# A graph network kernel: edge tables copied out of PSUM with group and side innermost, in place of the column

## The chip, the cores and the metric

The kernel runs on one core of one Trainium2 chip. The metric is the device time of one execution in microseconds (us). Three timed runs of the kernel before gave 2148.09, 2145.54 and 2143.85 us; the median is 2145.54 us.

The engines are called by the names that the profile uses: PE (matrix products), PEld (PE's weight loads), DVE (vector), ACT (scalar), POOL (GpSimd) and SP (which issues most DMAs).

## The reference, cut to what matters

Four graph layers run one after the other over 6250 nodes of 128 features, with a layer norm and a ReLU ahead of each. All of them sum over the same 206250 edges, sorted by destination:

```python
edge_index = jnp.stack([src, dst])
h = relu(layernorm(x)); x = x + L0(h, W1, b1, W2, b2, edge_weight, src, dst)   # weighted segment sum
h = relu(layernorm(x)); x = x + L1(h, edge_index, batch0, ...)                 # mean over incoming edges
h = relu(layernorm(x)); x = x + L2(h, x_clique, edge_index, W, b)              # mean of clique rows
h = relu(layernorm(x)); x = x + L3(h, edge_index, W_in, ..., W_out, b_out)     # gated update
# the sum over edges in each of them:
neighbor = jax.ops.segment_sum(edge_val[:, None] * x[edge_src], edge_dst, num_segments=N_NODES)
```

## The kernel before

The kernel does not gather a row for every edge. It builds the matrix of edge counts (and, for layer 0, of edge weights) between blocks of 128 nodes out of one-hot products on PE, writes the counts to DRAM, and multiplies the node rows by them. This has four parts in time: a setup, until about 146 us; the counting loop over 49 halves, until about 1174 us, which also finishes layer 0; the products of layers 1 and 2; and layer 3.

The change lies in the setup. Nodes are cut into groups of four (G). For every group there is a table entry for each edge, 128 edges from each of two sides (s = 0 counts from the group's first edge, s = 1 from its end). There are four tables, LO (low bits of the source), KEY (destination and high bits), WHI and WLO (the edge's weight in two f16 parts). They are made with the node group on the partitions and the edge along the row, and the counting loop wants the edge on the partitions. So `flip_groups` on PE multiplies every 128x128 square by the identity into PSUM, and `from_tab` copies it from PSUM (f32) to the table (f16). In PSUM, `p_tab[side]` lies as 7 groups x 2 sides x 128 columns, so one group and side is a run of 128 f32 (512 bytes). In the table the order is column n, then group g (13 of them, NGT), then side s: entries of one group and side that follow each other in n lie 13 x 2 f16, that is 52 bytes, apart.

The 13 groups go in two parts (TILES): part 0 has groups 0 to 6, part 1 has groups 7 to 12. `p_tab[0]` serves LO and WHI, which ACT copies (L1324, from the call ahead of `order_known` in the scalar block); `p_tab[1]` serves KEY and WLO, which DVE copies (L1722, `tables`). Each call of `from_tab` makes two copies: a small one of column 120 (14 elements a partition in part 0, 2 in part 1), and the main one of columns 0 to 119, with 120 x 7 x 2 = 1680 elements a partition in part 0 and 120 x 6 x 2 = 1440 in part 1. The small one is written with group and side as its only dimensions: it reads one f32 every 512 bytes and writes f16 in a row.

What sets the order around the change is code written by hand with semaphores. PE flips in the order LO, KEY, WHI, WLO of part 0, then the same of part 1 (L828). WHI may be flipped only when LO has been taken from `p_tab[0]` (`tab_taken0`), WLO only when KEY has been taken from `p_tab[1]` (`tab_taken1`), and so on in turns. ACT makes LO and WHI in f16 ahead (L1300, L1301), and has the layer norm of 24 blocks (L1317) between its two parts. DVE's list is: keys of part 0 (L1696 to L1702), KEY 0, WLO 0, keys of part 1, a check of the keys (L1708 to L1733), KEY 1, WLO 1, then `any_order` (L1736), and the semaphore `order_known`, which every engine waits for before it branches into the counting loop. POOL normalises the other 25 blocks (L731, L733); when it is done, SP stores the rows to DRAM (`node_rows`, L434).

Of the kernel before, what the change touches and what calls it, by code (L numbers as in the profile page):

```python
# [51 lines left out]
NGT = -(-NB * P // (G * P))  # L52
# [33 lines left out]
def build_gnn(nc, A, out):  # L86
    with ExitStack() as ctx:
# [209 lines left out]
        p_tab = [ps[:, n * 4 * TILE:n * 4 * TILE + 14 * P].rearrange("p (g s n) -> p g s n", g=7, s=2) for n in range(2)]  # L297
# [969 lines left out]
        def _(act):  # L1267
# [7 lines left out]
            def from_tab(write, tab, first, last, side):  # L1275

                full = NQUAD // NGT
                over = min(last, NQUAD - full * NGT) - first
                if over > 0:
                    write(tab[:, full * NGT * 2:].rearrange("p (g s) -> p g s", s=2)[:, first:first + over, :],  # L1280
                          p_tab[side][:, 0:over, :, full])
                t = tab[:, 0:full * NGT * 2].rearrange("p (n g s) -> p g s n", g=NGT, s=2)[:, first:last]
                return write(t, p_tab[side][:, 0:last - first, :, 0:full])

            act.wait_ge(sem("scan_ready"), 1)
            for g in SIGNED:
# [29 lines left out]
            for b in range(ACT_ROWS):  # L1316
                last = nc.scalar.activation(h0[:, b, :], h0[:, b, :], ACT.Relu, bias=shift0[:, b:b + 1],  # L1317
                                            scale=rstd0[:, b:b + 1])
            last.then_inc(sem("h0_ready"), 1)
            high_parts(1, *TILES[1])  # L1320
            for n, (first, last) in enumerate(TILES):
                for step, tab in ((0, LO), (2, WHI)):
                    act.wait_ge(sem("flipped"), n * 4 + step + 1)
                    from_tab(lambda t, v: nc.scalar.copy(t, v), tabs[tab], first, last, 0).then_inc(sem("tab_taken0"), 1)  # L1324
# [218 lines left out]
        def _(dve):  # L1543
# [139 lines left out]
            def from_tab(write, tab, first, last, side):  # L1683

                full = NQUAD // NGT
                over = min(last, NQUAD - full * NGT) - first
                if over > 0:
                    write(tab[:, full * NGT * 2:].rearrange("p (g s) -> p g s", s=2)[:, first:first + over, :],
                          p_tab[side][:, 0:over, :, full])
                t = tab[:, 0:full * NGT * 2].rearrange("p (n g s) -> p g s n", g=NGT, s=2)[:, first:last]  # L1690
                return write(t, p_tab[side][:, 0:last - first, :, 0:full])

            def keys(n, first, last):
                dve.wait_ge(sem(f"rec_in{n}"), 32 * (last - first))
# [24 lines left out]
            def tables(n, first, last):  # L1719
                for step, tab in ((1, KEY), (3, WLO)):  # L1720
                    dve.wait_ge(sem("flipped"), n * 4 + step + 1)
                    from_tab(lambda t, v: V.tensor_copy(t, v), tabs[tab], first, last, 1).then_inc(sem("tab_taken1"), 1)  # L1722
# [612 lines left out]
```

## Time and profile before

| what | value |
|---|---|
| timed runs, median | 2145.54 us |
| the profiled execution, its own time | 2161.86 us |
| its span on the core | 2159.9 us |
| granted PE clock, mean over the span | 0.96 |
| busy: PE, DVE, ACT, POOL | 1954.4, 1513.4, 1233.0, 140.3 us |
| share of the chain that ended last: PE, DVE, ACT | 81%, 6%, 5% |

The profiled execution took 16.3 us more than the median of the timed ones; its durations are read against its own span. Busy time is the time in which an engine has an instruction running; a busy PE is one whose queue of matmuls is not empty, and need not be at its peak. In the timeline, a row gives the start, the time, the engine, the line and the operation; rows of one line that follow each other are merged under the shape of the first (x2 means two instructions), and the bracket gives the idle time ahead and what ended it.

### The profile page before, as it was taken

How to read it: one execution, taken by the hardware profiler on the slowest of the kernel's cores; microseconds unless marked ns; L12 is line 12 of the kernel's file. 1: busy time of each engine (PE TensorE's matmuls, PEld its weight loads, DVE VectorE, ACT ScalarE, POOL GpSimd, SP SyncE). 2: the span in 40 equal slices, each digit the busy share in tenths (PEclk: the TensorE clock that was granted, in tenths of full speed). 3: DMA queues.
4: the chain of work that ended last, by engine and by line, in shares of the span. 5: the costliest groups of instructions: out<-in, count | busy, mean ns of one | idle time of the engine just before them, and what ended most of it. 6: DMA issues, size and time to landing. Idle time of an engine off the chain costs nothing.

```text
span 2159.9 us, 62665 instructions
## 1 busy us (share of the span) xinstructions
PE 1954.4 (90%) x22348; PEld 1769.7 (82%) x22393; DVE 1513.4 (70%) x3127; ACT 1233.0 (57%) x3189; POOL 140.3 (6%) x120
## 2 busy tenths in 40 slices
PE   1039999999999999999999899999999778999997
PEld 1039999999999999999999677777788766888854
DVE  8378888888888888888886666666887367100066
ACT  5456666666666666666665588888888543000043
POOL 4700000000000000000000000000000144000011
PEclk7559999999999999999999999999999989999999
DMA  8322222221222222121222433333487259998722
GB/s 229 91 61 96 74 101 91 83 100 73 100 73 101 84 91 100 73 100 73 100 77 103 164 140 132 134 130 136 159 316 257 69 163 348 369 315 300 267 83 77
DMA packets 184486, 304.21 MB, mean 141 GB/s; under 512 B 12642, under 2 KB 135959, under 8 KB 184175
## 3 DMA queue, kind: packets, MB, share of 16 engines
q1 hardware_dynamic: 180506, 290.74, 38.5%
q0 software_dynamic: 3904, 12.50, 1.9%
q8 instruction: 44, 0.72, 0.1%
q14 instruction: 32, 0.25, 0.0%
HBM read 202.70 MB, written 100.48 MB: 140 GB/s over the span
## 4 chain that ended last, share of the span: by engine, by line
PE 81%; DVE 6%; ACT 5%; issue 4%; DMA 2%; DVEq 1%; ACTq 0%; SPq 0%; POOLq 0%
PE ps L902 25%; PE ps L994 21%; PE ps L891 11%; PE ps L885 7%; PE ps L986 6%; PE ps L972 3%; PE ps L1183 2%; PE ps L1061 1%; ACT edge_area L1335 1%; PE ps L1158 1%; DMA hs<-node_rows 1%; PE ps L1069 1%; ACT edge_area L1288 1%; DMA edge_area<-x_stream 1%; DVE carry L1722 1%
## 5 line engine op out<-in xcount | busy, mean ns | idle before, releaser
L1335 ACT CAST edge_area<-ps 128x392 f16<-128x392 f32 x784 | 407.2, 519 | 393.1 <-PE ps L885 393.1
L902 PE MATMUL ps<-big,rows_area 128*128 128x128 f32 x4802 | 576.9, 277 | 0.0
L902 PEld LDWEIGHTS ps<-big,rows_area 128*128 128x128 f32 x4802 | 551.9, 192 | 0.0
L1341 ACT COPY big<-ps 128x392 f32<-128x392 f32 x784 | 416.9, 532 | 0.8 <-PE ps L891 0.5
L891 PE MATMUL ps<-edge_area 128*128 128x98 f16 x6272 | 416.7, 208 | 0.0
L1818 DVE TENSOR_TENSOR edge_area<-lo_pair,carry 128x1024 f16<-128x1024 f16 x392 | 269.2, 687 | 129.0 <-PE ps L891 125.4
L891 PEld LDWEIGHTS ps<-edge_area 128*128 128x128 f16 x6272 | 331.7, 97 | 0.0
L885 PE MATMUL ps<-edge_area 128*128 128x98 f16 x3136 | 276.3, 209 | 17.7 <-DVE edge_area L1824 11.0
L994 PE MATMUL ps<-big,agg 128*128 128x256 f16 (+1 forms) x2450 | 278.6, 271 | 0.0
L994 PEld LDWEIGHTS ps<-big,agg 128*128 128x128 f16 x2450 | 232.7, 98 | 25.3
L1819 DVE TENSOR_TENSOR edge_area<-cell_pair,carry 128x784 f16<-128x784 f16 x392 | 219.2, 559 | 0.0
L1824 DVE TENSOR_TENSOR edge_area<-edge_area,carry 128x784 f16<-128x784 f16 x392 | 219.0, 559 | 0.0
L1823 DVE TENSOR_TENSOR edge_area<-edge_area,carry 128x784 f16<-128x784 f16 x392 | 217.5, 555 | 0.1
L885 PEld LDWEIGHTS ps<-edge_area 128*128 128x128 f16 x3136 | 190.0, 98 | 33.6 <-ACT edge_area L1335 12.8
L1410 ACT ACTIVATE edge_area<-ps,edge_area 128x896 bf16<-128x896 f32 x175 | 167.0, 1003 | 75.4 <-PE ps L972 61.6
L1429 ACT ACTIVATE edge_area<-big 128x256 f16<-128x256 f16 (+1 forms) x504 | 201.0, 404 | 12.4 <-issue 2.6
L994 PE MATMUL ps<-big,rows_area 128*128 128x256 f16 (+1 forms) x1862 | 198.4, 270 | 0.0
L994 PEld LDWEIGHTS ps<-big,rows_area 128*128 128x128 f16 x1862 | 178.1, 98 | 20.1
L2070 DVE TENSOR_REDUCE out_part<-big 128x4 f32<-128x1024 f16 (+1 forms) x168 | 193.7, 1189 | 0.0
L2062 DVE TENSOR_TENSOR carry<-carry,ps 128x896 f32<-128x896 f32 x85 | 92.3, 1086 | 89.7 <-PE ps L986 89.7
L986 PE MATMUL ps<-edge_area 128*128 128x384 bf16 (+1 forms) x655 | 137.6, 351 | 3.6 <-DVE carry L2062 1.2
L2099 DVE TENSOR_SCALAR agg<-ps 128x256 f32 (+2 forms) x19 | 7.9, 418 | 180.2 <-PE ps L994 180.2
(253 smaller groups left out, 1793.1 us busy)
## 6 DMA issues: line engine op xcount, KB each, us to landing
big<-edge_counts SPq DMA_DIRECT2D x315, 448.0 KB, 5.2
edge_counts<-edge_area SPq DMA_DIRECT2D x49, 1568.0 KB, 5.6
agg<-edge_counts SPq DMA_DIRECT2D x21, 448.0 KB, 7.2
hs<-node_rows POOLq DMA_DIRECT2D x14, 448.0 KB, 4.3
edge_area<-x_stream SPq DMA_DIRECT2D x14, 448.0 KB, 4.3
node_rows<-rows_area SPq DMA_DIRECT2D x1, 3136.0 KB, 12.9
agg_s<-node_rows SPq DMA_DIRECT2D x49, 64.0 KB, 4.9
agg_s<-in_x SPq DMA_DIRECT2D x49, 64.0 KB, 1.8
```

Source lines behind the costliest of these rows:

```text
L885: last = mm(pair_of(p_count[s % 2], c), sources_of(slot, r, c), cells_of(oh_cell, slot, r, c), start=(c == 0), stop=(c == 3), skip_group_c ...
L891: last = mm(pair_of(p_weight[s % 4], c), sources_of(slot, r, c), cells_of(oh, slot, r, c), start=(c == 0 and oh is oh_whi), stop=(c == 3 a ...
L902: last = mm(p_sum, h0[:, n, :], w32[:, par, n, :], start=(n == 0), stop=(n == NB - 1))
L986: last = mm(p_mix[:, lo:hi], xc_plane[:, par, c, l, :], flipped[:, odd, c, lo:hi], start=(c == 0 and l == 0), stop=(c == parts - 1 and l = ...
L994: last = mm((p_block if l == 1 else p_even_odd)[par][:, 0:width, :], planes1[:, sh, p, :] if l == 1 else planes[:, p, sh, :], piece[:, par ...
L1335: nc.scalar.copy(store_slot[:, par, :, cols], p_count[s % 2]).then_inc(sem("count_taken"), 1)
L1341: nc.scalar.copy(w32[:, par, :, cols], p_weight[s % 4]).then_inc(sem("weight_taken"), 1)
L1429: last = nc.scalar.activation(unused[:, j, 0:width, :], piece[:, par, k, 0:width, j, :], ACT.Copy, accum_out=out_part[:, par, sh:sh + 1])
L1818: V.tensor_tensor(oh_src[:, slot], paired(lo_pair, P), lo.to_broadcast([P, 4, P, 2]), ALU.is_equal)
L1819: V.tensor_tensor(oh_cell[:, slot], paired(cell_pair, CELLS), key.to_broadcast([P, 4, CELLS, 2]), ALU.is_equal)
L1823: V.tensor_tensor(oh_whi[:, slot], oh_cell[:, slot], whi.to_broadcast([P, 4, CELLS, 2]), ALU.mult)
L1824: V.tensor_tensor(oh_wlo[:, slot], oh_cell[:, slot], wlo.to_broadcast([P, 4, CELLS, 2]), ALU.mult).then_inc(sem("onehots"), 1)
```

## The change

The main copy of `from_tab` takes its three dimensions in another order, on both engines that have it. Before, the column n is innermost: 120 f32 that lie in a row in PSUM are read, and each f16 is written 52 bytes after the one before it. After, group and side are innermost: an f32 is read every 512 bytes in PSUM, 14 of them (12 in part 1), and they are written as a run of 28 bytes (24 in part 1); then comes the next column, with the run 52 bytes further on. The elements, the bytes and the number of instructions are the same.

```diff
-                t = tab[:, 0:full * NGT * 2].rearrange("p (n g s) -> p g s n", g=NGT, s=2)[:, first:last]
-                return write(t, p_tab[side][:, 0:last - first, :, 0:full])
+                t = tab[:, 0:full * NGT * 2].rearrange("p (n g s) -> p n g s", g=NGT, s=2)[:, :, first:last, :]
+                return write(t, p_tab[side][:, 0:last - first, :, 0:full].rearrange("p g s n -> p n g s"))
```

The same two lines change in the scalar block (L1282 and L1283) and in the vector block (L1690 and L1691). No instruction changes its place. On DVE, in the setup between the keys of part 0 and those of part 1, the list differs only in the shape of the main copies (`carry` holds the tables, `ps` is PSUM):

```order
 L1702 SCALAR_TENSOR_TENSOR big<-edge_area,w_scale,big 128x1792
 L1722 CAST carry<-ps 128x14
-L1722 CAST carry<-ps 128x14x120
+L1722 CAST carry<-ps 128x120x14
 L1722 CAST carry<-ps 128x14
-L1722 CAST carry<-ps 128x14x120
+L1722 CAST carry<-ps 128x120x14
 L1696 TENSOR_SCALAR agg<-edge_area,first_key 128x256 x6
```

Nothing moved; eight copies in all (four on DVE, four on ACT) have this other shape.

## Rows read from the trace of the kernel before

**Rows 1.** Stretches: length, busy us of PE, PEld, DVE, ACT, POOL, PEclk, DMA share, GB/s.
```profile
100.00:141.00 41.00, 9.18 (x78) 8.22 (x78) 26.88 (x26) 28.98 (x9) 8.06 (x1) 0.54 0.28 79
141.00:146.00 5.00, 0.78 (x2) 0.49 (x2) 0.30 (x2) 0.00 (x0) 0.00 (x0) 0.50 0.03 7
170.00:1080.00 910.00, 904.58 (x12755) 891.50 (x12754) 794.97 (x1880) 570.33 (x1468) 0.00 (x0) 1.00 0.24 88
```

**Rows 2.** The timeline of the setup's end and the loop's first store, 98 to 166 us.
```profile
98.15 2.32 ACT L1301 ACTIVATE big<-edge_area,w_scale 128x1536 f16<-128x1536 f32 x1
100.39 7.64 ACT L1324 CAST carry<-ps 128x14 f16<-128x14 f32 x2
108.09 0.40 SPq L434 DMA_DIRECT2D node_rows<-rows_area  x1
108.17 3.08 PE L828 MATMUL ps<-ident,big 128*128 128x128 f16 x28 [20.76 <-ACT carry L1324]
109.86 7.67 ACT L1324 CAST carry<-ps 128x14 f16<-128x14 f32 x2 [1.83 <-PE ps L828]
111.29 7.70 DVE L1722 CAST carry<-ps 128x14 f16<-128x14 f32 x2 [14.08 <-PE ps L828]
117.68 1.44 PE L828 MATMUL ps<-ident,big 128*128 128x128 f16 x12 [6.43 <-ACT carry L1324]
121.64 2.31 DVE L1702 SCALAR_TENSOR_TENSOR big<-edge_area,w_scale,big 128x1536 f16<-128x1536 f32 x1
125.48 6.57 DVE L1722 CAST carry<-ps 128x2 f16<-128x2 f32 x2
132.20 1.44 PE L828 MATMUL ps<-ident,big 128*128 128x128 f16 x12 [4.77 <-DVE carry L1722]
133.67 6.57 DVE L1722 CAST carry<-ps 128x2 f16<-128x2 f32 x2 [1.62 <-PE ps L828]
145.99 0.69 DVE L1818 TENSOR_TENSOR edge_area<-lo_pair,carry 128x1024 f16<-128x1024 f16 x1 [3.40 <-issue]
165.38 0.40 SPq L454 DMA_DIRECT2D edge_counts<-edge_area  x1
```

**Rows 3.** Groups by line and shape, 0 to 140 us: the copies of the tables.
```profile
L1722 DVE CAST carry<-ps 128x1680 f16<-128x1680 f32 x2 | 15.3, 7628 | 0.0
L1324 ACT CAST carry<-ps 128x1680 f16<-128x1680 f32 x2 | 15.2, 7600 | 0.0
L1722 DVE CAST carry<-ps 128x1440 f16<-128x1440 f32 x2 | 13.0, 6501 | 0.0
L1722 DVE CAST carry<-ps 128x14 f16<-128x14 f32 x2 | 0.3, 162 | 14.1 <-PE ps L828 14.1
L1324 ACT CAST carry<-ps 128x14 f16<-128x14 f32 x2 | 0.3, 156 | 1.8 <-PE ps L828 1.8
L1722 DVE CAST carry<-ps 128x2 f16<-128x2 f32 x2 | 0.3, 154 | 1.6 <-PE ps L828 1.6
L1324 ACT CAST carry<-ps 128x2 f16<-128x2 f32 x2 | 0.3, 160 | 3.2 <-PE ps L828 3.2
```

**Rows 4.** Groups by line and shape: the nearest other copies, and two groups of the page.
```profile
L1300 ACT CAST big<-edge_area 128x1792 f16<-128x1792 f32 x1 | 2.6, 2636 | 4.7 <-DVE w_scale L1647 4.7
L1702 DVE SCALAR_TENSOR_TENSOR big<-edge_area,w_scale,big 128x1792 f16<-128x1792 f32 x1 | 2.7, 2669 | 1.6 <-ACT big L1301 1.6
L1410 ACT ACTIVATE edge_area<-ps,edge_area 128x896 bf16<-128x896 f32 x175 | 167.0, 1003 | 75.4 <-PE ps L972 61.6
L2062 DVE TENSOR_TENSOR carry<-carry,ps 128x896 f32<-128x896 f32 x85 | 92.3, 1086 | 89.7 <-PE ps L986 89.7
```

**Rows 5.** The DMA queues, 116 to 121 us: packets, MB, share of 16 engines.
```profile
q1 hardware_dynamic: 2373, 1.21, 84.8%
q8 instruction: 1, 0.02, 1.1%
```

**Rows 6.** DVE's instruction with the longest idle time put down to issue, 0 to 140 us.
```profile
L1639 DVE TENSOR_SCALAR hs<-hs 128x49 f32<-128x49 f32 x1 | 0.2, 191 | 8.3 <-issue 8.3
```

More of the change, by code:

```diff
@@ L1689, in from_tab @@
                           p_tab[side][:, 0:over, :, full])
-                t = tab[:, 0:full * NGT * 2].rearrange("p (n g s) -> p g s n", g=NGT, s=2)[:, first:last]
-                return write(t, p_tab[side][:, 0:last - first, :, 0:full])
+                t = tab[:, 0:full * NGT * 2].rearrange("p (n g s) -> p n g s", g=NGT, s=2)[:, :, first:last, :]
+                return write(t, p_tab[side][:, 0:last - first, :, 0:full].rearrange("p g s n -> p n g s"))
             def keys(n, first, last):
```

## The prediction
> **What bounds the kernel now.** I read the page first, then the stretches, then the timeline of the stretch in which the changed lines run. From 170 to 1080 us PE is busy 904.58 of 910 us at a granted clock of 1.00 (the level of 2.4 GHz) [rows 1]: the counting loop is PE's, and the change has no instruction in it. From 100 to 141 us no engine is full: PE 9.18, DVE 26.88, ACT 28.98 us of 41 [rows 1]. A stretch like this is a chain of waits between engines, and a microsecond taken from a link of it is a microsecond of the end, as everything after it starts by one semaphore. So the question is which copies are links.
>
> The timeline gives them [rows 2]. ACT copies LO 0 at 100.39 for 7.64 us; PE, idle for 20.76 us and released by this copy, flips WHI 0 and WLO 0 (28 matmuls, 3.08 us, to 111.25); DVE, idle for 14.08 us, copies WLO 0 at 111.29 for 7.70 us, to 118.99; DVE makes and checks the keys of part 1 until 125.48 (6.49 us); it copies KEY 1 (6.57 us, to 132.05); PE flips WLO 1 (12 matmuls from 132.20, 1.44 us); DVE copies WLO 1 at 133.67 for 6.57 us, to 140.24. Then come `order_known`, the branch, and the first one-hot of the loop at 145.99, 5.75 us later. Four of the eight main copies are links, with 7.64 + 7.70 + 6.57 + 6.57 = 28.48 us. The other four (KEY 0, WHI 0, LO 1, WHI 1) lie beside them.
>
> **What the change costs and brings, per copy.** The copy of 1680 elements takes 7628 ns on DVE and 7600 on ACT, that of 1440 takes 6501 [rows 3]. The slope between the DVE sizes is (7628 - 6501) / 240 = 4.70 ns an element; over the whole copy it is (7628 - 154) / 1680 = 4.45, with 154 ns as the fixed part (the copy of 2 elements). Both engines have the same slope, so it is not the engine's arithmetic; ACT copies out of PSUM in a row at (1003 - 156) / 896 = 0.95 ns and DVE at (1086 - 154) / 896 = 1.04 ns [rows 3, 4]. The reading of the slow copies is in a row too. What is left as the cause is the write of a lone f16 every 52 bytes, and that is what the edit removes.
>
> What it adds is a read of PSUM at one f32 every 512 bytes. The trace does show this read, once: the small copy of column 120 has just this pattern, 14 elements read 512 bytes apart and 28 bytes written in a row. It takes 162 ns on DVE against 154 for 2 elements, and 156 against 160 on ACT [rows 3]. That is 8 ns for 12 elements more, 0.7 ns each, and nothing on ACT. A step that cost 4.45 ns would have shown 53 ns. It is a short sample, and a queue could hide a cost in it, so I bound the rate from both sides: 0.95 to 1.04 ns as the floor (copies in a row), and 4.45 ns as the upper end (the row of the slow pattern itself). Between them lie the copies that read SBUF one f32 every 12 bytes: (2636 - 156) / 1792 = 1.38 ns on ACT, (2669 - 154) / 1792 = 1.40 on DVE [rows 4]. I take the floor, since the small copy is the nearest row and stands there. Below the floor I expect nothing: no copy out of PSUM in these rows is quicker than 0.95 ns an element, and the 0.7 of the small one comes from a difference of 8 ns.
>
> The new pairs, each with the small copy and its handover (0.04 us on ACT, 7.64 - 7.60; 0.07 on DVE, 7.70 - 7.63): LO 0 on ACT 0.156 + 1680 x 0.95 ns + 0.04 = 1.79; WLO 0 on DVE 0.154 + 1680 x 1.04 ns + 0.07 = 1.97; KEY 1 and WLO 1 0.154 + 1440 x 1.04 ns + 0.07 = 1.72 each. Sum 7.20 us, against 28.48: **21.3 us less** on the chain. In general the four links hold 6240 elements, so each nanosecond an element is worth 6.24 us, and the gain is about 6.24 x (4.45 - r).
>
> The Trainium skill has a rule that speaks against this much: its page "Vector Engine (DVE) Microarchitecture Reference" (section 5.2, Measured stream behaviour on trn2) says that a source that hops every element streams at 1.73 ns, not 1.05, and a destination that hops at 1.71, or 2.5 at a small step. It speaks of 32-bit words in SBUF. By it the gain is 6.24 x (4.45 - 1.73) = 17.0 us. This case's trace disagrees with it on the old pattern (4.45 ns for a hopping f16 destination), and the small copy's 0.7 ns speaks against it on the new one, in a sample of 14.
>
> **Do other links take over?** With LO 0 done at 102.18, the flips end at 105.4, WLO 0 at 107.4; keys and check are relative to it and end at 113.9, KEY 1 at 115.6, WLO 1 runs from 117.2 to 119.0. What else must be there: the WHI parts that DVE's keys use are made by 100.5 (ACT L1301), ahead of LO 0 on ACT; WHI 0 is copied by about 105.8, LO 1 by 109.2; the keys are there for PE at about 110.1 (before, 121.64, where L1702 begins, 2.65 us after WLO 0), so KEY 1 and WHI 1 are flipped by 113.2, ahead of 113.9 when DVE wants KEY 1, and WHI 1 is copied by 114.8, ahead of 119.0. KEY 0 sits in DVE's wait for the flips of WLO 0 (14.08 us idle), so its gain is worth nothing. The slack of the nearest one (KEY 1 flipped at 111.7 against 113.9) is 2 us, and holds.
>
> POOL's share of the layer norm and SP's store of the rows don't move: the store is issued at 108.09 [rows 2] and its packets still fill the DMA queues in most of 116 to 121 us [rows 5]. Before, the end of the chain came 19 us after that; now it comes 2 us before it. Who waits for the store is SP, whose first work in the loop was at 165.38 us [rows 2] and will be near 144; PE wants the normalised rows in the second half of the loop, which begins about then. Neither waits. What remains is the branch: the loop's code has to be fetched, by DMA, about 2.5 us after `order_known`, near 121.5, just behind the store. The first one-hot had 3.40 us of issue ahead of it with empty queues [rows 2]; the store's last packets could add to that, and DVE once stood 8.3 us for issue earlier in the setup [rows 6]. That is the upper end of what may be given back here, nothing is the lower one; the store should be through, so I charge 0.3.
>
> The sum for the profiled execution: 2161.86 - 21.3 + 0.3 = 2140.9 us. It lies 16.3 us above the median of the timed runs; the setup's chain has nothing that depends on that difference, so the same 21.0 us come off the median: 2145.5 - 21.0 = 2124.5 us.
>
> **Rivals.**
> 1. The read hop costs something: 1.4 ns an element, like the reads of every 12 bytes [rows 4], up to 2.5. For it: the sample that speaks against it has 14 elements, and runs of 28 bytes start at odd multiples of 4 bytes. Gain 6.24 x (4.45 - 1.4) = 19.0 at one end and 12.2 at the other: 2126.5 to 2133.3 us. The skill's 1.73 falls in here, as said.
> 2. The two steps are alike: PSUM read at 512 bytes costs as much an element as the scattered write did, 4.45 ns. The two engines' equal slopes would fit a memory's limit of either kind. Against: 53 ns would have shown in the small copy. Gain 0: 2145.5 us.
> 3. Slower: the bank of PSUM changes with every fourth element now (512 bytes each, 2 KB a bank), and a read that hops costs more than the write did. It decides from 4.45 ns on; at 6 ns the chain grows by 6.24 x 1.55 = 9.7 us, to 2155.2. Against it, again the small copy, which crosses the banks in the same way.
> 4. The copies do fall to 2 us, but the start of the loop is held by something that doesn't move: the fetch of the loop's code stands behind the row store. Price: the loop starts not at 124.8 but by the stall of [rows 6] later, up to 8.3 us: 2127 to 2133 us.
>
> **How the numbers follow.** Forecast 0.72 (2121 to 2127); rival 1 0.13; rival 4 0.07; rival 2 0.05; rival 3 0.03. A difference of under 0.2% (4.3 us) can't be told from no change here; the forecast and rivals 1 and 4 all lie beyond it. So faster 0.92, within it 0.05, slower 0.03. The range: down to 2119 for a floor that is lower by the spread of timed runs (4 us between the three), up to 2132, which takes in most of rivals 1 and 4.
>
> **What would show it.** In the profile after, the main copies at L1324 and L1722 stand at 1.6 to 1.9 us; PE's idle time ahead of the flips of WHI 0 falls from 20.76 to about 15 us; the first one-hot stands near 124.8; the counting loop and all that follows keep their durations, 21 us earlier. Copies of 2.5 to 4.5 us say rival 1; 7 us, rival 2; short copies with a gap of over 4 us at issue ahead of the first one-hot, rival 4. The forecast is wrong if the small copy's read is no sample of the long one's, or if the loop does not keep its length.

## The result, and the profile after

The changed kernel took 2132.53 us (median of four runs, 2130.87 to 2134.58) against 2146.82 us for the kernel before (four runs, 2143.85 to 2149.35): a ratio of 0.9934, with a 95% interval of 0.9917 to 0.9952. It is faster, by 14.3 us. The forecast was 21.0 us less, 2124.5 us, with a range up to 2132.0. The sign was right, and so was what the copies would gain; a third of the gain is missing at the end. Three single executions in the runs further down took 4.1 to 6.8 ms and stand in no ratio.

The copies are not where it is missing. The groups by line and shape of the changed kernel, 60 to 118 us, as in [rows 3], with the two groups that the text comes to below:

```profile
L1696 DVE TENSOR_SCALAR agg<-edge_area,first_key 128x256 f32<-128x256 f32 x13 | 12.2, 1004 | 4.7 <-DMA edge_area<-edge_records,edge_idx 4.7
L733 POOL TENSOR_SCALAR rows_area<-rows_area 128x3200 f32<-128x3200 f32 x1 | 8.5, 8457 | 3.5 <-issue 3.5
L1722 DVE CAST carry<-ps 128x1680 f16<-128x1680 f32 x2 | 3.8, 1900 | 0.0
L1722 DVE CAST carry<-ps 128x1440 f16<-128x1440 f32 x2 | 3.3, 1648 | 0.0
L1324 ACT CAST carry<-ps 128x1680 f16<-128x1680 f32 x2 | 3.1, 1567 | 0.0
```

DVE's copy of 1680 elements went from 7628 to 1900 ns (forecast 1.90 us), that of 1440 from 6501 to 1648 (forecast 1.65), ACT's from 7600 to 1567 (forecast 1.75). A read of PSUM at 512 bytes costs nothing that these rows show: (1900 - 154) / 1680 = 1.04 ns an element on DVE, the rate of its copies in a row, and (1567 - 156) / 1680 = 0.84 ns on ACT, which is less than the 0.95 ns that the forecast took as the floor. The small copy of 14 elements was a good sample. Rivals 1 to 3 fall.

The first row is the surprise: L1696, the first step of DVE's keys, has a mean of 1004 ns. The timeline of the changed kernel, 84 to 118 us, answers to [rows 2]:

```profile
84.47 1.61 ACT L1324 CAST carry<-ps 128x14 f16<-128x14 f32 x2
86.23 3.03 PE L828 MATMUL ps<-ident,big 128*128 128x128 f16 x28 [17.43 <-ACT carry L1324]
89.30 1.99 DVE L1722 CAST carry<-ps 128x14 f16<-128x14 f32 x2 [16.49 <-PE ps L828]
91.20 9.90 DVE L1696 TENSOR_SCALAR agg<-edge_area,first_key 128x256 f32<-128x256 f32 x6
92.20 8.46 POOL L733 TENSOR_SCALAR rows_area<-rows_area 128x3200 f32<-128x3200 f32 x1 [3.46 <-issue]
105.92 1.72 DVE L1722 CAST carry<-ps 128x2 f16<-128x2 f32 x2
107.78 1.44 PE L828 MATMUL ps<-ident,big 128*128 128x128 f16 x12 [2.77 <-DVE carry L1722]
109.25 1.73 DVE L1722 CAST carry<-ps 128x2 f16<-128x2 f32 x2 [1.62 <-PE ps L828]
117.32 0.69 DVE L1818 TENSOR_TENSOR edge_area<-lo_pair,carry 128x1024 f16<-128x1024 f16 x1 [3.31 <-issue]
```

The six key instructions of part 1 took 9.90 us, and of the 13 in the kernel one took 8407 ns, where the median is 382:

```profile
L1696 DVE TENSOR_SCALAR agg<-edge_area,first_key x13: 371/382/8407, 63.0 to 100.7; 128x256 f32<-128x256 f32 x13
```

That one, the fifth of the six, begins at 92.40 and ends at 100.81 us. POOL's long ReLU (L733, 8.46 us) runs from 92.20 to 100.66. The trace also shows something else: everything here is earlier than in the profile of before by more than the copies explain. LO 0 starts at 84.47, not at 100.39, although nothing ahead of it was changed.

### The profile page after: what moved, and what is told of

The parts are those of the page before. It is cut to its first block, busy times and chain, and to the rows that moved or that the text cites. A ratio compares the mean times of both kernels' runs of the same rounds, so it can differ in the third digit from the quotient of the medians.

```text
span 2130.3 us, 62710 instructions
## 1 busy us (share of the span) xinstructions
PE 1955.3 (92%) x22393; PEld 1766.6 (83%) x22393; DVE 1498.5 (70%) x3127; ACT 1210.8 (57%) x3189; POOL 140.0 (7%) x120
## 4 chain that ended last, share of the span: by engine, by line
PE 81%; DVE 5%; ACT 4%; issue 3%; DMA 3%; POOL 1%; DVEq 1%; ACTq 0%; POOLq 0%; SPq 0%
PE ps L902 26%; PE ps L994 21%; PE ps L891 11%; PE ps L885 7%; PE ps L986 6%; PE ps L972 3%; PE ps L1183 2%; POOL edge_area L724 1%; PE ps L1061 1%; ACT edge_area L1335 1%; PE ps L1158 1%; DMA hs<-node_rows 1%; PE ps L1069 1%; ACT edge_area L1288 1%; DMA edge_area<-x_stream 1%
## 5 line engine op out<-in xcount | busy, mean ns | idle before, releaser
L986 PE MATMUL ps<-edge_area 128*128 128x512 bf16 (+1 forms) x700 | 148.0, 354 | 1.2 <-DVE carry L2062 1.2
```

The lines of the kernel that those rows point to most:

```text
L986: last = mm(p_mix[:, lo:hi], xc_plane[:, par, c, l, :], flipped[:, odd, c, lo:hi], start=(c == 0 and l == 0), stop=(c == parts - 1 and l = ...
```

## The experiments

**The kernel before, profiled again.** The same program was run and profiled four more times, to see what the setup of a 2146 us run looks like.

> The kernel before, unchanged, profiled a second time. Theory 1 (the keys of part 1 now meet POOL's long ReLU): the first profile of before had 23 us of DVE issue gaps at L1637 to L1645 that the timed runs do not have, so layer-norm scales come at about 58 us instead of 81; the chain is then set by the record gathers (landed about 80), LO 0 starts about 84.5, WLO 0 ends about 103, the keys of part 1 take about 6.5 us because POOL's L733 ended at about 100.7, and the first one-hot stands at about 130; L1696 of part 1 at 0.4 us each. Theory 2 (the time is given back at the branch or later, not at the keys): the keys of part 1 take as long as in the changed kernel, about 14 us, or the first one-hot stands at 138 or later. Time 2146 us in both.

> The kernel before, for its profile beside the kernels of this call. Theory 1: if its time is near 2146 us, layer-norm scales come at about 58 us without issue gaps, LO 0 starts near 84.5, WLO 0 ends near 103 when POOL's long ReLU is over (100.7), all L1696 are under 0.6 us, and the first one-hot stands near 130. Theory 2: an L1696 of several us is there too, so the ReLU is no new wait of the change. If its time is near 2162 us, the profile is as the first one.

> The kernel before, for its profile beside the kernels of this call; as for before_third: beside times near 2146 us the first one-hot near 130 with all L1696 under 0.6 us (theory 1), or with one of several us (theory 2).

> The kernel before, for its profile. Theory 1: beside times near 2146 us the first one-hot near 130, all L1696 under 0.6 us; theory 2: one L1696 of several us. Beside times near 2162 us as before_third.

Measured: 2162.22, 2161.41, 2162.41 and 2146.15 us. The setup is found in two conditions, whatever the kernel, and kernels that ran side by side were always in the same one (on one and the same chip both were met at different times). In the one, DVE waits for issue again and again from L1637 to L1645, as in [rows 6], and the layer-norm scales come at about 80 to 83 us: I call it *late scales*. It is that of the profile on which the prediction rests. In the other the scales come at 58 us: *early scales*. It is that of the timed runs. The timeline of before with early scales (before_fifth), 57 to 131 us:

```profile
57.75 0.21 DVE L1645 SCALAR_TENSOR_TENSOR hs<-hs 128x49 f32<-128x49 f32 x1
84.37 7.63 ACT L1324 CAST carry<-ps 128x14 f16<-128x14 f32 x2
92.18 8.31 POOL L733 TENSOR_SCALAR rows_area<-rows_area 128x3200 f32<-128x3200 f32 x1 [3.46 <-issue]
95.33 7.75 DVE L1722 CAST carry<-ps 128x14 f16<-128x14 f32 x2 [16.94 <-PE ps L828]
102.65 2.06 DVE L1696 TENSOR_SCALAR agg<-edge_area,first_key 128x256 f32<-128x256 f32 x6
109.58 6.56 DVE L1722 CAST carry<-ps 128x2 f16<-128x2 f32 x2
117.77 6.57 DVE L1722 CAST carry<-ps 128x2 f16<-128x2 f32 x2 [1.62 <-PE ps L828]
130.07 0.69 DVE L1818 TENSOR_TENSOR edge_area<-lo_pair,carry 128x1024 f16<-128x1024 f16 x1 [3.38 <-issue]
```

Here the keys of part 1 begin at 102.65, two microseconds after the ReLU's end (100.49), and take 2.06 us. So before, they never met it: with late scales neither, where the ReLU ended at 108.06 and the keys began at 118.59. The first one-hot stands at 130.07, as expected. DVE's waits for issue account for the late scales: 21.9 us of them from L1637 to L1645 in the first profile, none in before_fifth, and scales 23.5 us apart (81.28 and 57.75). What makes them come at some times and not at others was not found.

**The changed kernel in both conditions.**

> The changed kernel, unchanged, beside the others. The last four runs showed a kernel before at 2162 us with DVE waiting for issue at L1637 and L1639 (layer-norm scales at 82 us), where the result's runs had 2146 us and no such waits (scales at 58 us). Theory 1 (what the change gives depends on where POOL's long ReLU lies against the keys of part 1): beside a before of 2162 us the gain is the full sum of links less the last 1 us of the ReLU, 20 to 21 us (2141.5 us), with all L1696 under 0.6 us or one of about 1.2; beside a before of 2146 us it is 13 to 15 us (2132.5 us), with one L1696 of about 8 us. Theory 2 (about 7 us are given back wherever the copies are short): 14 us in both.

> The changed kernel once more. Theory 1: beside a before near 2162 us it gains 20 to 21 us (2141.5 us), the keys of part 1 meeting only the last microsecond of POOL's ReLU; beside one near 2146 us again 13.5 us (2132.5 us). Theory 2: 14 us in both.

Measured: with early scales 2132.89 us against 2146.55 (0.9936, interval 0.9922 to 0.9950), 13.7 us; with late scales 2142.06 against 2163.18 (0.9900, 0.9883 to 0.9916), 21.1 us. The second is the forecast's gain. That it agrees to a tenth is luck, as its interval is some 7 us wide, but the first one-hot moved by as much, 20.8 us (146.72 in before_fourth, 125.96 here). In the trace of after_third, 100 to 126 us, the keys begin in the ReLU's last microsecond (it ends at 108.65) and lose 0.6 us to it (2.62 us against 2.01 in before_fourth):

```profile
100.34 8.31 POOL L733 TENSOR_SCALAR rows_area<-rows_area 128x3200 f32<-128x3200 f32 x1 [3.46 <-issue]
107.68 2.62 DVE L1696 TENSOR_SCALAR agg<-edge_area,first_key 128x256 f32<-128x256 f32 x6
115.13 1.71 DVE L1722 CAST carry<-ps 128x2 f16<-128x2 f32 x2
125.96 0.69 DVE L1818 TENSOR_TENSOR edge_area<-lo_pair,carry 128x1024 f16<-128x1024 f16 x1 [3.38 <-issue]
```

**The ReLU twice.** The changed kernel, with (`...` marks what is cut from a line)

```diff
-            nc.gpsimd.tensor_scalar(h0[:, ACT_ROWS:NB, :], ..., 0.0, None, ALU.max).then_inc(sem("h0_ready"), 1)
+            nc.gpsimd.tensor_scalar(h0[:, ACT_ROWS:NB, :], ..., 0.0, None, ALU.max)
+            pool.drain()
+            nc.gpsimd.tensor_scalar(h0[:, ACT_ROWS:NB, :], ..., 0.0, None, ALU.max).then_inc(sem("h0_ready"), 1)
```

> The changed kernel with POOL's long ReLU (L733) done twice over; the second pass changes no value. Theory 1: DVE's L1696 of part 1 stands still until the second pass is over, so the whole kernel is 8 to 9 us slower than after_again beside it, and one L1696 of 8 us (before of 2162 us) or of 16 us (before of 2146 us) is seen. Theory 2 (the long L1696 was a wait for gathered records or for DVE's own pipe, not POOL): POOL is 20 us off the chain, so no change.

Measured: 2142.23 us, 9.3 us over after_again, which ran beside it (early scales); the first one-hot stands at 125.81 against 116.83. DVE's keys (here L1698) stand for both passes:

```profile
91.62 17.90 DVE L1698 TENSOR_SCALAR agg<-edge_area,first_key 128x256 f32<-128x256 f32 x6
92.47 8.31 POOL L733 TENSOR_SCALAR rows_area<-rows_area 128x3200 f32<-128x3200 f32 x1 [3.46 <-issue]
100.94 8.44 POOL L735 TENSOR_SCALAR rows_area<-rows_area 128x3200 f32<-128x3200 f32 x1 [0.15 <-issue]
```

DVE's keys wait for one semaphore that POOL has a part in, that of the gathers, and these were issued and landed earlier: the last was issued at 77.02 us in the changed kernel, and in keys_early, below, the same six instructions are done at 82.77. Nothing ties them to the ReLU. So it is the instructions themselves that exclude each other: two stood for 8.4 us each, one beside either pass, and one got through in the gap of 0.15 us between the passes. This settles the cause. It does not hold for every instruction of DVE. Its copies out of PSUM keep their length beside the same ReLU, 7.75 us at 95.33 in before_fifth above, and in keys_early:

```profile
94.75 8.31 POOL L733 TENSOR_SCALAR rows_area<-rows_area 128x3200 f32<-128x3200 f32 x1 [3.46 <-issue]
95.69 1.72 DVE L1722 CAST carry<-ps 128x2 f16<-128x2 f32 x2 [1.62 <-PE ps L828]
```

In the Trainium skill, "SBUF — State Buffer" (section SBUF: two separate sides) says that VectorE and GpSimd share a port pair, which a VectorE instruction takes only in a two-port mode or with two SBUF inputs, and that whichever starts first keeps it for the whole instruction while the other fully blocks. The trace agrees with the block: 8407 ns of DVE beside 8457 ns of POOL. In which mode L1696 ran, no run here shows.

**The layer norm's share off POOL.** The changed kernel, with POOL's L731 and L733 taken out and done by DVE behind KEY 0:

```diff
+                    if n == 0 and step == 1:
+                        for b in range(ACT_ROWS, NB):
+                            V.tensor_scalar(h0[:, b, :], h0[:, b, :], rstd0[:, b:b + 1], shift0[:, b:b + 1], ALU.mult, ALU.add)
+                        dve.drain()
+                        V.tensor_scalar(h0[:, ACT_ROWS:NB, :], ..., 0.0, None, ALU.max).then_inc(sem("h0_ready"), 1)
```

> The changed kernel with POOL's 25 blocks of layer norm and its long ReLU (L731, L733) moved to DVE, right behind KEY 0, where DVE is idle for 16 us; result the same. Theory 1: L1696 of part 1 back at 0.4 us each, keys of part 1 in about 6.5 us instead of 14.6, first one-hot near 109.5 instead of 117.3, time 2124.5 us, which is what was forecast for the change. Theory 2: the keys stay slow, or what they gain is lost at the branch; 2132.5 us.

> The changed kernel with POOL's share of the layer norm and its long ReLU moved to DVE behind KEY 0, a second time, since the first run stood beside a before of 2162 us, where the keys meet no ReLU. Theory 1: beside a before of 2146 us it is 7.5 to 8.5 us under the changed kernel, 2124.5 to 2125 us, which is the forecast for the change; no L1696 over 0.6 us, first one-hot near 109. Theory 2: 2132.5 us.

> The changed kernel with POOL's blocks and ReLU on DVE. Theory 1: beside a before near 2146 us 2124.5 to 2125 us, 8 us under the changed kernel; beside one near 2162 us within 1.5 us of the changed kernel, since there is next to nothing of the ReLU to meet there. Theory 2: it is 7 us or more under the changed kernel in both, or in neither.

> The changed kernel with POOL's blocks and ReLU on DVE. Theory 1: beside a before near 2146 us 2124.5 to 2125 us, 21.5 us under before and 8 us under the changed kernel; theory 2: 2132.5 us. Beside a before near 2162 us 2142 to 2143 us a fourth time.

> The kernel before with the same move of POOL's blocks and ReLU to DVE. Theory 1: before, the keys of part 1 come after the ReLU's end, so there is nothing to win: within 1 us of before (DVE's extra 8.5 us lie in its idle time ahead of WLO 0). Theory 2 (the move helps by itself, for instance by the earlier store of rows or by less sharing of a port elsewhere): several us under before.

Measured with late scales: 2143.86, 2142.25 and 2143.14 us, the last beside after_third's 2142.06: nothing to win there. With early scales (norm_on_dve_4): 2127.74 us against 2146.12 (0.9910, interval 0.9895 to 0.9924), 5.2 us under after_again (whose before had 2146.55), where 8 were expected. The same edit on the kernel before gave 2164.29 against 2162.66 (1.0013, 1.0004 to 1.0022), late scales: nothing won, and 1.6 us lost where at most 1 was expected. The trace of norm_on_dve_4 (DVE's keys at L1690, its copies at L1716):

```profile
79.40 1.83 DVE L1721 TENSOR_SCALAR rows_area<-rows_area 128x3200 f32<-128x3200 f32 x1
91.55 1.89 DVE L1690 TENSOR_SCALAR agg<-edge_area,first_key 128x256 f32<-128x256 f32 x6
98.26 1.72 DVE L1716 CAST carry<-ps 128x2 f16<-128x2 f32 x2
108.99 0.69 DVE L1818 TENSOR_TENSOR edge_area<-lo_pair,carry 128x1024 f16<-128x1024 f16 x1 [3.28 <-issue]
```

The whole gain is back at the start of the loop: 130.07 - 108.99 = 21.1 us before before_fifth, against the forecast's 21.3 for the links. What is left of the way is longer, though: from the first one-hot to the end of the span 2126.0 - 109.0 = 2017.0 us, against 2129.8 - 116.8 = 2013.0 in after_again. The counting loop is not where: from its first one-hot to its last it takes 1020.5 us in both. The difference opens in layer 3, at POOL's first additions there and at DVE's L2222, which waits for them. Here are these rows of after_again, then of norm_on_dve_4 (where POOL's lines lie 6 higher up):

```profile
1717.69 2.09 POOL L787 TENSOR_TENSOR big<-big,shift 128x896 f32<-128x896 f32 x1 [0.84 <-issue]
1722.12 1.09 DVE L2222 TENSOR_TENSOR big<-big 128x896 f32<-128x896 f32 x1 [0.36 <-POOL big L790]
```

```profile
1713.83 2.08 POOL L781 TENSOR_TENSOR big<-big,shift 128x896 f32<-128x896 f32 x1 [4.10 <-issue]
1718.25 1.09 DVE L2222 TENSOR_TENSOR big<-big 128x896 f32<-128x896 f32 x1 [3.62 <-POOL big L784]
```

POOL stands 4.10 us for issue ahead of that addition, not 0.84, and DVE 3.62 us for POOL, not 0.36: 3.3 of the 4.0 us. Every profile in which POOL's two lines are taken out has 4.10 there (seven, before_norm_on_dve and the two with keys early among them), and every other has 0.84. So the edit pays for its 7.8 us in the setup with some 3 us in layer 3; why POOL's issue takes longer there was not found.

**One engine at a time.**

> Only ACT's two lines changed (LO and WHI), DVE's copies as before. Theory 1: LO 0 is 6.0 us shorter, but then the keys of part 1 begin near 97 and stand still until POOL's long ReLU ends at 100.7; net gain 2 to 3 us, 2144 us. Theory 2 (no meeting of keys and ReLU): the gain is the whole 6.0 us of the link, 2140.5 us.

> Only DVE's two lines changed (KEY and WLO), ACT's copies as before. Theory 1: WLO 0, KEY 1 and WLO 1 give 5.7 + 4.8 + 4.8 = 15.3 us, of which 3 to 4 us are lost as the keys of part 1 begin near 97.4 and wait for POOL's long ReLU to end at 100.7; net 12 us, 2134.5 us, so that both halves together (12 + 2.5) are about what the whole change gave, 14.3 us, and not the 21.3 us of the sum of links. Theory 2: 15.3 us, 2131.5 us, no slower than the whole change.

Measured, both with late scales (before 2162.32 us): only ACT 2156.21 us (0.9973, 0.9963 to 0.9983), 6.1 us; only DVE 2154.15 us (0.9967, 0.9956 to 0.9978), 8.2 us. Expected were 2.5 and 12, for early scales. ACT alone gives its one link, with no ReLU in the way at that hour. DVE alone gives 8.2 us (5.4 at the first one-hot, 146.60 to 141.20) and not 15.3, since ACT's old copies, until then beside the chain, become links; the timeline of dve_only, 117 to 142 us:

```profile
120.49 6.59 ACT L1324 CAST carry<-ps 128x2 f16<-128x2 f32 x2 [1.62 <-PE ps L828]
121.77 1.72 DVE L1722 CAST carry<-ps 128x2 f16<-128x2 f32 x2 [0.45 <-PE ps L828]
127.23 2.72 PE L828 MATMUL ps<-ident,big 128*128 128x128 f16 x24 [5.49 <-ACT carry L1324]
129.99 1.73 DVE L1722 CAST carry<-ps 128x2 f16<-128x2 f32 x2 [6.49 <-PE ps L828]
141.20 0.69 DVE L1818 TENSOR_TENSOR edge_area<-lo_pair,carry 128x1024 f16<-128x1024 f16 x1 [3.45 <-issue]
```

PE's flips wait 5.49 us for ACT's LO 1. The halves give 14.3 us together, the whole 21.1 in the same condition: a link that is shortened alone can hand the chain to a copy beside it.

**Keys ahead of WLO 0.** Two versions that could beat both kernels, here the cut of the edit that turns the order (`tables` takes the steps as an argument; the second version also has the edit above):

```diff
-            tables(0, *TILES[0])
+            tables(0, *TILES[0], steps=((1, KEY),))
             keys(1, *TILES[1])
+            tables(0, *TILES[0], steps=((3, WLO),))
```

> The changed kernel with DVE's order turned: keys of part 1 ahead of the copy of WLO 0, in DVE's idle time. Theory 1: the keys leave the chain and don't meet the long ReLU behind WLO 0; beside a before of 2146 us the first one-hot stands near 104 instead of 117 (2119 us), beside one of 2162 us near 120 instead of 125 (2136 us). The rival: PE's fixed order of flips or ACT's copies take over at once and nothing is gained, 2132.5 or 2141.5 us.

> The changed kernel with the keys of part 1 ahead of WLO 0 and POOL's blocks and ReLU on DVE ahead of them. keys_early had its first one-hot 13.6 us sooner, but ACT's first copy of the loop then stood 7 to 8 us for the semaphore that SP raises only after the store of the rows has landed, and only 5.2 us were left of it. Theory 1: with the ReLU done by 81 us the store lands by 95, nothing is held, and the whole 13 us come through: beside a before of 2146 us 2119 us, beside one of 2162 us near 2136 us. The rival (DVE's list is now too long, or the loop's code comes later): 2124 us or more.

> The changed kernel with keys early and POOL's blocks and ReLU on DVE. Theory 1: beside a before near 2146 us 2119 us; beside one near 2162 us again 2138 us. The rival: nothing under norm_on_dve_3.

Measured: keys_early, early scales, 2127.71 us (0.9910 to before, 0.9895 to 0.9925), 5.2 us under after_again. Its first one-hot stands at 103.19, 13.6 us sooner, but the loop then stops; the waits of the stretch 100 to 160 us name the reason, with the row of SP's store from the timeline behind:

```profile
ACT edge_area L1335 <- SPq L527: 22.5, 1, 22.5
DVE edge_area L1819 <- PE ps L891: 10.6, 4, 7.5
```

```profile
103.09 0.40 SPq L434 DMA_DIRECT2D node_rows<-rows_area  x1
```

ACT's first copy of the loop waits for `half_saved0`, which SP raises behind its wait for the store of the rows; the store's last packets moved at about 115.2 and ACT started at 117.38. With the layer norm on DVE as well the store is done long before: 2138.21 and 2138.56 us with late scales (0.9889 and 0.9887 to before), 3.5 us under after_third and the fastest version in that condition. With early scales it was not run, so its expected 2119 us is untested.

**Runs of 4 bytes.** The kernel before, with side alone innermost:

```diff
-                t = tab[...].rearrange("p (n g s) -> p g s n", g=NGT, s=2)[:, first:last]
+                t = tab[...].rearrange("p (n g s) -> p g n s", g=NGT, s=2)[:, first:last]
```

> The kernel before with side innermost only (group, column, side): PSUM is read 512 bytes forth and back, and f16 pairs of 4 bytes are written every 52 bytes. Theory A (the cost is one of each separate place written): half as many places, so about 2.2 ns an element and a main copy of 1680 at 3.8 us. Theory B (each f16 write costs 4.45 ns unless the next is in the same longer line): pairs don't help fully, over 3 ns an element. Theory C (the cost is of a 2-byte write that does not fill a 4-byte word): full pairs cost what a lone f32 write costs at a step of 12 bytes or less, 1.4 ns, main copy 2.4 us.

Measured: 2133.50 us, beside 2132.89 for after_again, and copies as short as in the changed kernel:

```profile
L1722 DVE CAST carry<-ps 128x1680 f16<-128x1680 f32 x2 | 3.8, 1900 | 0.0
L1324 ACT CAST carry<-ps 128x1680 f16<-128x1680 f32 x2 | 3.2, 1606 | 0.0
```

All three theories missed the time (the nearest, of full pairs, had 2.4 us). Two f16 in a row, every 52 bytes, cost 1.04 ns each on DVE; one alone cost 4.45. So the lone write was the price of the old copies, and the 28 bytes are not what matters: a pair is enough. Whether it is enough because it fills an aligned word of 4 bytes, as all pairs here do, or because two follow each other, no run here tells apart.

## Why the prediction was wrong, point by point

- *Which copies are links, and their old and new lengths.* Right. With early scales the four links went from 7.63, 7.75, 6.56 and 6.57 us to 1.61, 1.99, 1.72 and 1.73, which is 21.5 us (forecast 21.3). PE's idle time ahead of the flips of WHI 0 fell from 20.76 to 14.55 in after_third, where about 15 was forecast. (LO 0 on ACT went under the floor, 1.61 us where 1.79 was forecast.)
- *Price of the read at 512 bytes.* Right, the floor. The 1.73 ns that the Trainium skill has for a source that hops ("Vector Engine (DVE) Microarchitecture Reference", section 5.2, measured in SBUF) does not carry over to this read of PSUM, which took 1.04 ns. Rival 1's runs at odd multiples of 4 bytes are every second run only, as they lie 52 bytes apart; it made no difference.
- *"Keys and check are relative to it", 6.49 us.* This is the step that failed. The stretch from WLO 0's end to KEY 1 took 6.50 us in before_fifth (103.08 to 109.58) and 14.63 in the changed kernel (91.29 to 105.92): 8.1 us, POOL's ReLU. From WLO 1's end to the first one-hot the way took 6.3 us instead of 5.7, so 0.6 more, where 0.3 were charged. 21.5 - 8.1 - 0.6 = 12.8 us, which is what the first one-hot moved (130.07 to 117.32). The medians moved by 13.7 and 14.3 us; the microsecond or so between that and 12.8 is within the spread of single executions.
- *"The setup's chain has nothing that depends on that difference"* (of 16.3 us between the profiled execution and the median). This let the step fail. The difference was the setup's own: 15.9 us of first one-hot between the two profiles of before (145.99 and 130.07). In the profiled condition POOL's ReLU ended just as WLO 0 did (108.06 and 107.4 as forecast), and the gain was indeed 21.1 us; in the timed one, WLO 0 ends 9.1 to 9.4 us ahead of the ReLU's end.
- *"POOL's share of the layer norm doesn't move"* was true and the trouble: I checked who waits for POOL by semaphore, and not what runs beside it.
- *Who waits for the store of rows.* Half right: no wait here, but the claim that SP's first work in the loop is near 144 us overlooked that ACT needs SP's semaphore at the loop's start (keys_early, 7.5 us).
- *Rival 4* had the right kind, new copies short and the loop held by something that doesn't move, in the right range (2127 to 2133 us), with the wrong place. That the result lies in its range is luck: the gap at issue ahead of the first one-hot, which it wanted over 4 us, was 3.31.

## What to carry to other kernels

When a chain is shortened, lay the new times of its instructions over what other engines run at those times, and not only over the semaphores: two instructions without any dependence can still exclude each other, as the one of 382 ns did that took 8407. When the profiled execution differs from the timed ones by almost as much as the gain in question, first find the stretch of the difference, since the engines' phases there are other than in the runs that will be timed. And test a waiting theory by doubling the suspected blocker: 8.4 us of harmless work gave 9.3 us.

## What the runs showed of the hardware

- A lone f16 written every 52 bytes costs 4.45 ns on DVE and ACT alike; as a pair of 4 bytes 1.04 ns on DVE ((1900 - 154) / 1680). Reads of PSUM at 512 bytes run at 1.04 ns an element on DVE, as fast as its copies in a row, and at 0.84 ns on ACT.
- A DVE instruction of 0.38 us stood 8.4 us beside one GpSimd instruction of 8.3 to 8.5 us, and again for a second one. DVE's copies out of PSUM kept their length beside it (1.72 us).
- DVE's issue gaps in the layer norm's statistics (21.9 us or none) come or stay away for all kernels that run side by side, on the same chip at different times, and move the first one-hot by some 16 us. Why was not found.
- POOL stood 4.10 us for issue at its first addition of layer 3 in every kernel that has two of its instruction lines less in the setup, and 0.84 us in every other. Why was not found.
